# Softplus corrections as accumulating transfers in a state-space stage, and ScalarE's share for the next chunk cut into halves

## The reference

```python
x_and_res = x @ W_in                      # 256 -> 2 * 512
xc, res = split(x_and_res)
xconv = causal convolution of xc over time, 4 taps, + conv_b
xs = silu(xconv)
dt_r, Bm, Cm = split(xs @ W_x)            # 64, 16, 16
dt = softplus(dt_r @ W_dt + b_dt)
h_t = exp(dt_t * A) * h_(t-1) + dt_t * Bm_t * xs_t      # 512 x 16 states, over 2048 steps
y = (h_t . Cm_t) + xs * D
out = (y * silu(res)) @ W_out
```

## Time and profile before

| | us |
|---|---|
| median of 3 runs | 3249.03 (3243.03 to 3251.33) |
| the profiled execution, its own time | 3247.61 |
| its span in the profile | 3245.9 |
| VectorE busy in the span | 2649.6 (82%) |
| TensorE busy | 2899.3 (89%) |
| ScalarE busy | 1707.3 (53%) |
| GpSimd busy | 979.8 (30%) |
| scans in the state-space stage, 512 | from 248.4 to 1245.1 |

### The profile page before, as it was taken

One profiled execution on the slowest core, in us unless ns is written; L12 is line 12 of the kernel. 1 busy time (PEld: TensorE's weight loads), 2 busy tenths in 40 slices (PEclk: granted clock), 3 DMA queues, 4 the chain that ended last, 5 costly groups with the idle time before them and its releaser, 6 DMA issues. The chain is left out here.

```text
span 3245.9 us, 44528 instructions
## 1 busy us (share of the span) xinstructions
PE 2899.3 (89%) x13148; PEld 1475.8 (45%) x13148; DVE 2649.6 (82%) x4268; ACT 1707.3 (53%) x2088; POOL 979.8 (30%) x554
## 2 busy tenths in 40 slices
PE   5768889898898774999999999999999999859998
PEld 3423344344343332444444444444444443548887
DVE  8819999999999995898998989899999995642222
ACT  3435565564555541276776767676767778101111
POOL 3515565565565565010101101011010000343443
PEclk9889999999999887699999989999999999769999
DMA  6731122121221214654355535555454520555663
GB/s 202 183 105 53 72 72 92 61 83 71 78 85 52 85 58 58 81 78 65 61 71 83 82 48 73 71 83 84 56 76 57 70 42 19 100 138 186 208 202 113
DMA packets 206638, 288.69 MB, mean 89 GB/s; under 512 B 113437, under 2 KB 154038, under 8 KB 191948
## 3 DMA queue, kind: packets, MB, share of 16 engines
q1 hardware_dynamic: 195052, 260.22, 38.1%
q0 software_dynamic: 11360, 25.62, 2.7%
HBM read 237.34 MB, written 53.36 MB: 90 GB/s over the span
## 5 line engine op out<-in xcount | busy, mean ns | idle before, releaser
L786 DVE TENSOR_REDUCE attn_mx<-attn_pX 128x1 f32<-128x512 f32 (+1 forms) x2560 | 1306.0, 576 | 112.5 <-PE attn_pX L691 72.0
L762 ACT ACTIVATE attn_pr<-attn_pS 128x1024 f32<-128x1024 f32 x1024 | 992.6, 1022 | 488.4 <-PE attn_pS L703 487.6
L691 PE MATMUL attn_pX<-attn_ks,attn_qs 48*128 48x512 f32 (+1 forms) x2560 | 904.9, 431 | 48.0 <-DMA attn_vs<-v_d 25.6
L691 PEld LDWEIGHTS attn_pX<-attn_ks,attn_qs 48*128 48x128 f32 x2560 | 449.9, 191 | 676.8 <-DVE attn_mx L786 581.0
L1225 PE MATMUL mamba_pY<-mamba_g,mamba_ident 128*128 128x512 f32 x1024 | 516.4, 651 | 138.5 <-DVE mamba_g L1373 138.3
L1353 DVE TENSOR_TENSOR_SCAN mamba_h<-mamba_pA,mamba_hs,mamba_db 128x512 f32<-128x512 f32 x512 | 616.7, 1263 | 12.7 <-ACT mamba_pA L1075 12.4
L703 PE MATMUL attn_pS<-attn_qs,attn_ks 50*128 50x512 f32 x2048 | 597.5, 452 | 23.3 <-issue 19.9
L1011 POOL TENSOR_TENSOR mamba_db<-mamba_bq,mamba_u 128x2048 f32<-128x2048 f32 x128 | 579.9, 4530 | 60.9 <-DVE mamba_u L1314 60.9
L1075 ACT ACTIVATE mamba_pA<-mamba_dt,held_an 128x512 f32<-128x512 f32 x512 | 352.6, 692 | 390.4 <-DVE mamba_h L1353 390.1
L713 PE MATMUL attn_pO<-attn_pr,attn_vs 128*17 128x512 f32 x4096 | 551.6, 611 | 0.5 <-ACT attn_pr L762 0.4
L1225 PEld LDWEIGHTS mamba_pY<-mamba_g,mamba_ident 128*128 128x128 f32 x1024 | 201.3, 206 | 442.7 <-DVE mamba_g L1373 227.4
(11 more groups left out here) (200 smaller groups left out, 2097.5 us busy)
## 6 DMA issues: line engine op xcount, KB each, us to landing
mamba_bq<-bc_d SPq DMA_DIRECT2D x64, 1024.0 KB, 4.7
attn_ks<-parts_d SPq DMA_DIRECT2D x192, 256.0 KB, 9.5
exp_w<-in_w SPq DMA_DIRECT2D x46, 1024.0 KB, 5.6
attn_vs<-v_d SPq DMA_DIRECT2D x32, 544.0 KB, 15.9
parts_d<-proj_qp SPq DMA_DIRECT2D x32, 512.0 KB, 3.9
attn_qs<-parts_d SPq DMA_DIRECT2D x192, 64.0 KB, 8.3
oraw_d<-attn_oe SPq DMA_DIRECT2D x32, 256.0 KB, 2.1
v_d<-proj_vs SPq DMA_DIRECT2D x32, 136.0 KB, 4.2
```

Of the source, the lines that this page charges most:

```text
L691: pe.matmul(pX[bank(s, e)][:, 0:width], QS[slot][rows, pair, qt * P:(qt + 1) * P], KS[slot][rows, pair, keys:keys + width], start=True, st ...
L762: act.activation(PR[2 * (kt % 2) + pair][:, :, :], pS[pair][:, :, :], ACT.Exp, scale=HD ** -0.5).then_inc(p_sb, 1)
L786: dve.tensor_reduce(MX[:, col, a:a + 1], pX[bank(s, e)][:, 0:width], AX.X, ALU.max).then_inc(x_max, 1)
```

## The change

For every chunk but the first, the six corrections of VectorE (two roundings, two subtractions, two additions per chunk) go. In their place:
- ScalarE makes the negative of the rounding in two passes: `soft_one` (1 + e) and `soft_lost` (1 - that). With U' = 1 - (1 + e), dt = relu + e + U' + ln(1 + e): DT, which holds relu, receives E, U' and LN one behind the other, each added by a transfer that accumulates into its destination. The logarithm goes to a new tile LN.
- GpSimd issues these transfers, `add_steps`: 128 x 1024 each (512 KB, 4 KB per partition), three for each half, behind DB of units 11 to 15, two of them in unit 14. Each waits for its source and for the transfer before it in the same half.
- VectorE keeps only `times_x`, in units 14 and 15, and waits there for the third transfer of that half.
- ScalarE's Silu and logarithm are cut into halves: Silu in units 4 and 6, logarithm in units 13 and 14. Some passes move to a second place in the unit, behind decay 3 (`soft_exp`, `soft_lost`, `soft_one` and the convolution copy of the chunk after the next, which goes from unit 15 to 14 and waits for the first transfer of half 0).
- The first chunk keeps VectorE's corrections, with the logarithm in two halves.

```diff
@@ GpSimd
+                def add_steps(c, s2, half, src, n):
+                    rows = slice(2 * half, 2 * half + 2)
+                    if n < 2:
+                        pool.wait_ge(soft_e, c * 6 + (3 * half + 2 * n + 5))
+                    else:
+                        pool.wait_ge(soft_done, c * 2 + (half + 3))
+                    if n > 0:
+                        pool.wait_ge(dt_sum[half], c * 48 + 16 * n)
+                    pool.sem_inc(waited_pool, 1)
+                    pool.dma_start(DT[s2][:, rows, :], src[:, rows, :], accum_op=ALU.add).then_inc(dt_sum[half], 16)
...
+                        if k == 11 and not last:
+                            add_steps(c, 1 - s, 0, E, 0)
+                        if k == 12 and not last:
+                            add_steps(c, 1 - s, 0, U[1 - s], 1)
+                        if k == 13 and not last:
+                            add_steps(c, 1 - s, 1, E, 0)
+                        if k == 14 and not last:
+                            add_steps(c, 1 - s, 0, LN, 2)
+                            add_steps(c, 1 - s, 1, U[1 - s], 1)
+                        if k == 15 and not last:
+                            add_steps(c, 1 - s, 1, LN, 2)
@@ ScalarE
-                    act.activation(XS[:, :, :], E[:, :, :], ACT.Silu).then_inc(xs_done, 1)
+                    act.activation(XS[:, rows, :], E[:, rows, :], ACT.Silu).then_inc(xs_done, 1)
...
+                def soft_lost(c, s2, half):
+                    rows = slice(2 * half, 2 * half + 2)
+                    act.wait_ge(soft_e, c * 6 + 3 * half)
+                    act.activation(U[s2][:, rows, :], U[s2][:, rows, :], ACT.Identity, bias=1.0, scale=-1.0
+                                   ).then_inc(soft_e, 1)
+                def soft_log(half):
+                    rows = slice(2 * half, 2 * half + 2)
+                    act.activation(LN[:, rows, :], E[:, rows, :], ACT.Ln, bias=1.0).then_inc(soft_done, 1)
...
+                        if k == 4 and not last:
+                            act.wait_ge(skipped, c + 1)
+                            act.wait_ge(u_done, c * 2 + 2)
+                            conv_silu(use + X1, 0)
                         if k == 6 and not last:
-                            act.wait_ge(skipped, c + 1)
-                            act.wait_ge(u_done, c * 2 + 2)
-                            conv_silu(use + X3)
+                            conv_silu(use + X3, 1)
...
+                        if k == 11 and not last:
+                            soft_one(c + 1, s2, 0)
+                        if k == 12 and not last:
+                            soft_exp(use + DT0 + 3, 1)
                         if (k == 11 or k == 12) and not last:
-                            half = k - 11
-                            soft_exp(use + DT0 + 3, c + 1, s2, half)
-                            for j in (2 * half, 2 * half + 1):
+                            for j in (2 * k - 22, 2 * k - 21):
                                 gate_in(use + Z0 + j, 11 + j, s2, s2, j)
-                        if k == 13 and not last:
-                            soft_log(c + 1)
+                        if (k == 13 or k == 14) and not last:
+                            soft_log(k - 13)
                         if k == 15 and not last:
                             gate_silu(use + Z0 + JT - 1, s2)
-                            if more:
-                                act.wait_ge(dt_done, c * 2 + 3)
-                                conv_out(use + USES + X0, 0, s, 0)
                         decay(c, s, k, 2)
                         decay(c, s, k, 3)
+                        if k == 10 and not last:
+                            soft_exp(use + DT0 + 1, 0)
+                        if k == 11 and not last:
+                            soft_lost(c + 1, s2, 0)
+                        if k == 12 and not last:
+                            soft_one(c + 1, s2, 1)
+                        if k == 13 and not last:
+                            soft_lost(c + 1, s2, 1)
+                        if k == 14 and more:
+                            act.wait_ge(dt_sum[0], c * 48 + 16)
+                            conv_out(use + USES + X0, 0, s, 0)
@@ VectorE
+                    if first:
+                        dve.wait_ge(dt_done, half + 1)
+                    else:
+                        dve.wait_ge(dt_sum[half], c * 48)
...
-                        if (k == 11 or k == 12) and not last:
-                            rounding(c + 1, 1 - s, k - 11)
-                        if k == 13 and not last:
-                            less_lost(c + 1, 1 - s, 0)
-                            plus_relu(c + 1, 1 - s, 0)
-                        if k == 14 and not last:
-                            times_x(c + 1, 1 - s, 0)
-                            less_lost(c + 1, 1 - s, 1)
-                        if k == 15 and not last:
-                            plus_relu(c + 1, 1 - s, 1)
-                            times_x(c + 1, 1 - s, 1)
+                        if (k == 14 or k == 15) and not last:
+                            times_x(c + 1, 1 - s, k - 14)
```

More of the change, by code:

```diff
@@ L888, in phase_mamba @@
         dt_done = m.sem("dt_done")
+        dt_sum = [m.sem(f"dt_sum{half}") for half in range(2)]
         u_done = m.sem("u_done")
@@ L1013, in body @@
                                            ).then_inc(db_done, 1)
+                        if k == 11 and not last:
[9 more added lines that the diff above has]
+                            add_steps(c, 1 - s, 1, LN, 2)
                 bodies(pool, body)
+                for half in range(2):
+                    pool.wait_ge(dt_sum[half], 48 * (NCH - 1))
             @block.scalar
@@ L1056, in soft_exp, with soft_one, steps_ready @@
                     act.activation(E[:, rows, :], E[:, rows, :], ACT.Exp, scale=-1.0).then_inc(soft_e, 1)
[L1057 removed]
+                    act.wait_ge(soft_e, 2 * half + 1)
+                    act.activation(U[0][:, rows, :], E[:, rows, :], ACT.Identity, bias=1.0
+                                   ).then_inc(soft_e, 1)
+                def soft_exp(use, half):
+                    rows = slice(2 * half, 2 * half + 2)
+                    act.wait_ge(p_sb, use + 1)
+                    act.activation(E[:, rows, :], E[:, rows, :], ACT.Exp, scale=-1.0).then_inc(soft_e, 1)
+                def soft_one(c, s2, half):
+                    rows = slice(2 * half, 2 * half + 2)
+                    act.wait_ge(soft_e, c * 6 + (3 * half - 1))
                     act.activation(U[s2][:, rows, :], E[:, rows, :], ACT.Identity, bias=1.0
                                    ).then_inc(soft_e, 1)
[L1061 to L1064 removed]
+                def soft_lost(c, s2, half):
+                    rows = slice(2 * half, 2 * half + 2)
+                    act.wait_ge(soft_e, c * 6 + 3 * half)
+                    act.activation(U[s2][:, rows, :], U[s2][:, rows, :], ACT.Identity, bias=1.0, scale=-1.0
+                                   ).then_inc(soft_e, 1)
+                def soft_log(half):
+                    rows = slice(2 * half, 2 * half + 2)
+                    act.activation(LN[:, rows, :], E[:, rows, :], ACT.Ln, bias=1.0).then_inc(soft_done, 1)
+                def steps_ready(c, half, first):
+                    if first:
+                        act.wait_ge(dt_done, half + 1)
+                    else:
+                        act.wait_ge(dt_sum[half], c * 48)
                 def mo_copy(c, place, par, n):
@@ L1079, in _ @@
                     conv_out(X0 + j, j, 0, j)
-                conv_silu(X3)
+                for half in range(2):
+                    conv_silu(X3, half)
                 low_rank(WXU, 6, 0, 0, first=True)
@@ L1084, in _ @@
                         dt_in(DT0 + j, 7 + j, 0, 0, j)
-                    soft_exp(DT0 + 2 * half + 1, 0, 0, half)
-                soft_log(0)
+                    soft_first(DT0 + 2 * half + 1, half)
+                act.wait_ge(lost_s, 2)
+                for half in range(2):
+                    soft_log(half)
                 for j in range(JT):
@@ L1098, in body @@
                         if k == 0 or k == 2:
-                            act.wait_ge(dt_done, c * 2 + (1 + k // 2))
+                            steps_ready(c, k // 2, first)
                         decay(c, s, k, 0)
@@ L1339, in _ @@
                 for half in range(2):
-                    rounding(0, 0, half)
+                    rounding(half)
                 for half in range(2):
-                    less_lost(0, 0, half)
-                    plus_relu(0, 0, half)
-                    times_x(0, 0, half)
+                    less_lost(half)
+                    plus_relu(half)
+                    times_x(0, 0, half, first=True)
                 def body(c, u, s, first, last, more):
```

40 lines of the change are left out of this document (19 added, 21 removed).

## The result

| | before | after |
|---|---|---|
| median of the runs, us | 3247.62 (3243.03 to 3251.33, 4 runs) | 3202.95 (3199.74 to 3205.95, 4 runs) |
| the profiled execution, own time / span | 3247.61 / 3245.9 | 3200.37 / 3198.6 |
| state-space stage, first product G to last | 992.0 | 944.6 |
| VectorE busy in the span | 2649.6 | 2607.0 |
| ScalarE busy | 1707.3 | 1757.1 |

The ratio is 0.9857, 95% interval [0.9843, 0.9871]: 1.4% shorter, clear of the noise. The profiled execution fell by 47.24 us and the state-space stage by 47.4, so the gain lies in that stage. The other stages, whose code is the same, moved by a few us each and nearly cancelled: attention (first to last maximum) was 3.0 shorter, what follows it 4.6 longer, and the first product G came 1.0 earlier.

The account below looks back on a forecast made before the run. VectorE was taken to bound the state-space stage, busy 123.79 of 126 us per chunk, TensorE not far behind. 6.89 per chunk times seven gives 48.2: 3247.6 - 48.2 + 3.5 = 3202.9, plus 1.4 to the median: 3204, range 3193 to 3232.

Parts of the forecast that it names:

- the term of 3.5 us for TensorE: State-space stage: TensorE's 115.09 us per chunk must fit in 119.1; a clock dip costs 0.5 per chunk, 3.5 in all.
- Removed from VectorE: Corrections leave VectorE in the state-space stage: units 11 and 12 save 1.09 us each, unit 14 1.14, unit 15 1.27.
- Rival 5: VectorE's removed work in the state-space stage was hidden anyway: no change, 3249 us; chance 0.03.
- ScalarE in pieces: Silu and logarithm in halves: unit 6 saves 0.85 us, unit 4 loses 0.55, unit 13 saves 2.00.
- The second place: ScalarE's place behind a unit's fourth exponential: a pass there costs nothing, with 2.7 us for 1.06 and 0.69.
- Issues: GpSimd's six transfer issues per chunk, 0.78 us each, fit its 2.38 us of waiting per unit and cost nothing.
- rival 2: GpSimd's issues are held until VectorE's product G ends: 2.6 us per chunk, 18 in all, 3222; chance 0.07.
- the narrow reading: VectorE's two-input operations block only GpSimd operations that read SBUF, so GpSimd's transfer issues are not held.
- Landing: Time from a transfer's issue to its landing: 4.7 to 5.7 us, under every limit.
- the limit of 8.6: Half 0's first transfer: landing time beyond which GpSimd's next DB is late, 7.05 plus 1.6 us.
- Rival 1: Transfers land somewhat late, at 9 us: 2.55 us per chunk, 18 in all, 3222; chance 0.13.
- Rival 3: Accumulating is several times slower than copying: even at landings of 10.0 us, 3305 us at 12; chance 0.09.

Follow-up runs that it names:

- last_sum_on_vector: Changed kernel with the last of each half's three additions back on VectorE, two transfers per chunk fewer: ratio 0.9937 to the kernel before, stage 965.4 us.
- gpsimd_adds: Changed kernel with the six additions per chunk as GpSimd's own operations in place of transfers: 3272.42 us, ratio 1.0097 to the kernel before.
- load_one_later: Changed kernel with the 1 MB load that starts with half 0's first transfer put one unit later: ratio 0.9836 to the kernel before, stage 946.9 us.
- one_transfer: Changed kernel with one accumulating transfer per half (only the logarithm) in place of three: ratio 0.9846 to the kernel before, stage 944.4 us.
- copies_not_sums: Changed kernel with the six transfers per chunk overwriting DT in place of adding to it: ratio 0.9843 to the kernel before, stage 943.6 us.
- last_transfer_late: Changed kernel with the last transfer of half 0 issued one unit later: 3255.33 us, ratio 1.0052 to the kernel before.

## Why the prediction was right

Predicted 3204, measured 3202.95. That the two are 1 us apart is in part luck: the runs themselves spread over 6 us, the term of 3.5 us for TensorE did not come true, and the late landings that did come were in no term. The sum for the stage is the fairer test: 48.2 us predicted, 47.4 measured. By its steps:

- **Removed from VectorE.** Unit 11 came to 7.05, units 14 and 15 to 8.63 and 8.64, as predicted. `last_sum_on_vector` and `gpsimd_adds` show from both sides that work on VectorE, or shown inside it, makes the stage longer (by 20.8 and 80.5 us). Rival 5 is out.
- **ScalarE in pieces.** Units 4 and 6: 7.59 and 7.60 against 7.60. The wait is 0.44 each and not 0.55 as a wait; the unit's length is as predicted. In unit 13 its price of 0.55 is there once the cover is taken away. The second place costs nothing where the passes stand now; without it, 0.9 per chunk are lost.
- **Unit 10.** In the chunk shown it fell from 7.27 to 7.05, which is in no term. It is no gain of the change: in both kernels some chunks have 7.3 there (four before, three after) and the others 7.05 to 7.12.
- **Issues.** A single one takes 0.86 against 0.78 taken; those close behind other work of GpSimd's queue show up to 1.22. The issue at 684.38 ran beside the G at 684.33 without a hold on either, so rival 2 is out and the narrow reading stands. With 1.2 us in unit 14 they still fit into GpSimd's idle time.
- **Landing, the step that was mis-sized.** I took 4.7 to 5.7 "under every limit above", and dismissed the 1 MB load beside the first transfer since such loads land in 4.7. Measured 4.6/7.5/9.8, and 8.6 to 9.05 for the first transfer against the limit of 8.6; the 0.56 or more from landing to the issue that waited for it was in no term. Rival 1's mechanism did occur. It cost unit 12 0.59 in the chunk shown and 0.7 in the mean. Transfer and load make each other late, and moving the load away brings the first transfer to 4.5, as `load_one_later` shows. The last transfer of half 1 has a load beside it too, 8.2 in the middle, and in one chunk VectorE waited 0.25 for it.
- **Why that did not show.** While G waits in unit 12, ScalarE catches up, and the 0.55 that it would have cost in unit 13 is gone. Units 12 and 13 came to 15.28 where 15.25 was predicted; over seven chunks to 15.46 against 15.27 without the hold, 0.19 per chunk or 1.3 us in all. Two waits one behind the other on different engines cost little more than one of them. `one_transfer`, `copies_not_sums` and `load_one_later` take the first away and each finds the second in its place.
- **Rival 3** is out: its break-even was 10.0 for all transfers, and the middle of the landings is 7.5, the most 9.8. `last_transfer_late` shows the cliff: 8.6 us per chunk for one transfer past its limit.
- **TensorE.** 3.5 us were taken for a dip of its clock, and its waits did not grow: the gate products waited 5.1 against 5.4. In the chunk shown the granted clock was 1.00, the full level, where it was 0.96 before, so its work took 110.24 of 118.69 us and not 115.09. The term should have been nothing in this execution. The measured fall of the profiled execution, 47.24, lies between the sum without it, 48.2, and with it, 44.7.

## What to carry to other kernels

Where two engines get into each other's way, work is only moved off one of them if it lands on neither: the same additions as transfers gained 47 us and on GpSimd lost 33 against the kernel before. Before you rely on a transfer, look at what else starts on the same event, and compute the limit for each waiting instruction, the issuing engine's own among them. Look at each place by itself: the middle over all transfers, 7.5, hid that one with no load beside it landed in 4.6 and the three with one in 8 to 9. When you remove a wait, ask which one it covered: here 0.59 on one engine hid 0.55 on another, and taking the first away alone brought 1.3 us at most.

## What the runs showed of the hardware

- An accumulating transfer from SBUF to SBUF of 512 KB (4 KB per partition) takes about twice a copy's time on the transfer engines (2.1 by these shares). GpSimd's queue had 2.7% of 3245.9 us before and 6.2% of 3198.6 after, 110.7 us more for 42 transfers, 2.6 each over all 16 engines; as copies (4.4% of 3189.2) 52.7 us, 1.25 each. The Trainium skill ("Collectives: The Full Stack", section on the bandwidth ceiling) says that an added sum takes a second source read and halves the rate; the runs agree. The bytes of the queue's line count each transfer once, 47.65 MB either way.
- With no load beside it and no earlier one under way, such an accumulate landed 4.5 to 4.7 us after its issue, the copy 2.9 to 3.0. The first of a chunk, with a 1 MB load starting within 0.1 us of it, took 8.6 to 9.05 as an accumulate and 6.8 to 7.0 as a copy. The load was late as well: 5.8 to 7.7, 6.4 in the middle, for the 20 beside an accumulate, against 4.7 in the middle of the other 44 (changed kernel).
- Of two accumulates issued 0.55 us apart the first landed in 4.6 and the second in 6.6 (changed kernel); with a 1 MB load beside them, 8.7 and 10.7 (`last_transfer_late`).
- From such a landing to the start of the GpSimd issue that waited for it 0.56 to 0.61 us went by.
- Issuing an accumulate shows 0.84 to 1.22 us on GpSimd, a copy of the same tiles 0.54 to 0.59.
- An operation with two SBUF inputs on GpSimd and one on VectorE exclude each other, in both directions, and the first to start takes its own time: GpSimd's addition of 128 x 1024 took 2.35 when it was first and 4.46 when G was, and G 4.30 and 2.29.
- A change in one stage made another, untouched stage 27 to 39 us longer, on two chips. TensorE's stops at that stage's loop turns grew by 27.0 and 28.0 us, and the instruction traffic of one queue from 0.85 to 1.11 MB.
